# Row additions by chunk, normalisations in halves and a later transpose in the feed-forward stages of a cross-attention kernel

## The reference

```python
# layer 0: two cross attentions, then
h = _layer_norm(x, ln_mlp_scale, ln_mlp_offset)
h = gelu(h @ w_fc1 + b_fc1) @ w_fc2 + b_fc2          # 256 -> 1024 -> 256
return x + h
...
# layer 1: cross attention with latents, then
out = rmsnorm(attn_out, postnorm_w)
out = gelu(out @ mlp_w1 + mlp_b1) @ mlp_w2 + mlp_b2
return out + residual
...
# layer 2: cross attention, then
y = layer_norm(hidden, ln2_w, ln2_b)
return hidden + (gelu(y @ fc_w + fc_b) @ proj_w + proj_b)
...
# layer 3: attention over features, batch norm over all tokens, + x
```

## Time and profile before

| | |
|---|---|
| median of 3 timed runs | 1546.92 us (1546.78 to 1547.07) |
| the profiled execution's own time | 1547.88 us |
| its span, first to last instruction | 1546.1 us |
| TensorE busy | 1505.0 us, 97% |
| VectorE busy | 966.5 us, 63% |
| ScalarE busy | 872.6 us, 56% |
| Pool busy | 416.3 us, 27% |
| mean granted TensorE clock | 0.994 |

### The profile page before, as it was taken

How to read it: one execution, slowest core, us unless ns; L and a number is a source line. 1 busy time by engine, 2 the same in 40 slices (tenths; PEclk the granted TensorE clock), 3 DMA queues, 4 the chain that set the end, 5 groups by cost and what they waited for, 6 DMA issues and landing times. The chain is left out here.

```text
span 1546.1 us, 41347 instructions
## 1 busy us (share of the span) xinstructions
PE 1505.0 (97%) x17435; PEld 1314.3 (85%) x17435; DVE 966.5 (63%) x2125; ACT 872.6 (56%) x1635; POOL 416.3 (27%) x449
## 2 busy tenths in 40 slices
PE   9999999999999899999999999999999999999996
PEld 8888888888898788888888888978878988888864
DVE  7755564555666464645655576389996567865366
ACT  6563454454356454453353566577776667765476
POOL 3420210210211510210210124046764206542052
PEclk9999999999999899999999999999999999999998
DMA  6010010010010010010010000020002000001001
GB/s 216 29 43 2 28 43 1 29 42 2 29 42 2 28 42 2 29 43 2 29 43 29 29 9 21 1 84 2 4 28 83 1 29 3 30 2 28 9 21 55
DMA packets 17832, 46.20 MB, mean 30 GB/s; under 512 B 1360, under 2 KB 11616, under 8 KB 14704
## 3 DMA queue, kind: packets, MB, share of 16 engines
q1 hardware_dynamic: 13456, 39.33, 7.3%
q10 hardware_dynamic: 4192, 4.24, 0.8%
HBM read 39.37 MB, written 4.19 MB: 28 GB/s over the span
## 5 line engine op out<-in xcount | busy, mean ns | idle before, releaser
L174 PE MATMUL ps<-ch,W 128*128 128x512 f32 (+1 forms) x2517 | 583.0, 381 | 3.1 <-DVE ch L603 0.9
L174 PEld LDWEIGHTS ps<-ch,W 128*128 128x128 f32 x2517 | 439.0, 189 | 86.8 <-issue 2.2
L174 PEld LDWEIGHTS ps<-W,split_arena 128*128 128x128 f32 x3084 | 388.4, 188 | 23.5 <-issue 5.2
L174 PE MATMUL ps<-W,split_arena 128*128 128x256 f32 x3084 | 402.0, 283 | 3.3 <-DVE split_arena L1729 2.4
L1382 DVE TENSOR_REDUCE small<-ps 128x4 f32<-128x260 f32 x128 | 53.9, 421 | 240.5 <-PE ps L776 240.5
L1223 ACT ACTIVATE arena<-ps,hbias 128x512 f32<-128x512 f32 x128 | 87.8, 689 | 206.3 <-PE ps L174 205.3
L174 PE MATMUL ps<-W,ch 128*128 128x512 f32 (+1 forms) x1002 | 195.6, 353 | 0.4
L1208 ACT ACTIVATE arena<-ps 64x256 f32<-64x256 f32 x256 | 97.0, 379 | 170.1 <-PE ps L875 166.3
L174 PEld LDWEIGHTS ps<-W,ch 128*128 128x128 f32 x1002 | 162.5, 189 | 26.5 <-ACT arena L2217 0.9
L1729 DVE TENSOR_TENSOR split_arena<-arena,split_arena 128x512 fp32r<-128x512 f32 x96 | 72.2, 752 | 125.2 <-ACT split_arena L1761 115.5
L1409 DVE TENSOR_TENSOR x_sb<-ps,x_sb 128x512 f32<-128x512 f32 x128 | 86.5, 689 | 94.5 <-PE ps L174 94.4
(11 more groups left out here) (173 smaller groups left out, 2021.4 us busy)
## 6 DMA issues: line engine op xcount, KB each, us to landing
raw<-wpack SPq DMA_DIRECT2D x23, 1028.0 KB, 4.8
rows<-vb_in SPq DMA_DIRECT2D x8, 512.0 KB, 5.7
x_sb<-x_in SPq DMA_DIRECT2D x4, 512.0 KB, 9.6
arena<-ctxT SPq DMA_DIRECT2D x4, 512.0 KB, 10.1
spill<-x_sb ACTq DMA_DIRECT2D x1, 2048.0 KB, 11.7
arena<-spill ACTq DMA_DIRECT2D x1, 2048.0 KB, 9.4
arena<-ctx_tok SPq DMA_DIRECT2D x16, 128.0 KB, 2.1
out<-x_sb SPq DMA_DIRECT2D x7, 256.0 KB, 2.5
```

The costliest lines, as they stand in the source:

```text
L174: last = e.matmul(dst, lhs[a], rhs[b], start=start and n == 0, stop=stop and n == 2, skip_group_check=True)
```

## The change

Three things change, in stage 0 and stage 2 of the feed-forward stages.

1. Pool's row additions. Before, Pool took the power and the row addition of one chunk as a pair, in the first chunk of the stage. Now the powers come first, and the row addition of chunk c (all but chunk 0 of stage 0, and chunks 2 and 3 of stage 2) waits for the low part of the first unit of chunk c. The row of chunk 0 in stage 0 comes after the power of chunk 1.
2. In stage 0 the normalised rows `x` of chunks 2 and 3 are made in two halves, with a unit's low part between them.
3. In stage 0 the transposes of chunk 3 come a unit later (after "down" of unit 9, not of unit 8), and with them their evacuation, high part and low part.

```diff
@@ end of pool_attend
-            norm0.pool(e, 0, row("b_fc2"), 2)
+            norm0.pool_pow(e, 0, 2)
@@ mlp: own_norm, stage 0 (FT is 8)
-                {"dve": {1: [("x", 1)], 4: [("stats", 2)], 5: [("lo", 1), ("x", 2)],
-                         6: [("stats", 3)], 7: [("x", 3)], FT: [("lo", 2)], FT + 3: [("lo", 3)]},
-                 "pe": {3: [("T", 1)], 6: [("T", 2)], FT: [("T", 3)]},
+                {"dve": {1: [("x", 1)], 4: [("stats", 2)], 5: [("lo", 1), ("x_a", 2)],
+                         6: [("x_b", 2), ("stats", 3)], 7: [("x_a", 3)], FT: [("x_b", 3), ("lo", 2)], FT + 4: [("lo", 3)]},
+                 "pe": {3: [("T", 1)], 6: [("T", 2)], FT + 1: [("T", 3)]},
                  "act": {4: [(0, 1), (1, 1)], 5: [(2, 1), (3, 1)], 7: [(0, 2), (1, 2)], FT: [(2, 2), (3, 2)],
-                         FT + 1: [(0, 3), (1, 3)], FT + 2: [(2, 3), (3, 3)]}},
+                         FT + 2: [(0, 3), (1, 3)], FT + 3: [(2, 3), (3, 3)]}},
@@ mlp: pool(e, c, first, last)
                 if first and which == 0:
-                    for j in range(1, NCH):
-                        norm.pool(e, j, row(out_row), l)
+                    norm.pool_pow(e, 1, l)
+                    norm.pool_row(e, 0, row(out_row), l)
+                    norm.pool_pow(e, 2, l)
+                    norm.pool_pow(e, 3, l)
+                elif which == 0:
+                    e.wait_ge(s["gl"].sem, s["gl"].at(c * FT))
+                    norm.pool_row(e, c, row(out_row), l)
...
                 if first and which:
                     for j in range(front.left, NCH):
-                        norm.pool(e, j, norm.row)
+                        norm.pool_pow(e, j)
+                if which and norm.row is not None and c >= front.left:
+                    e.wait_ge(s["gl"].sem, s["gl"].at(c * FT))
+                    norm.pool_row(e, c, norm.row)
```

## The result

The changed kernel takes 1549.22 us (median of 22 runs, 1547.94 to 1549.96) against 1546.92 before (22 runs, 1546.15 to 1547.76): a ratio of 1.0013 [1.0007, 1.0019], taken over all runs (the two medians alone give 1.0015). It is 2.3 us slower, within the 0.2% that I called the same, but outside the range and on the other side of before than the predicted 1546.5.

The account below looks back on a forecast made before the run. TensorE, busy 1505.0 of 1546.1 us, was taken to bound the kernel, so only its waits could be gained. The terms 0.4 - 0.1 + 0.15 = 0.45 us took 1546.92 to 1546.5, range 1545.2 to 1547.9.

Parts of the forecast that it names:

- (a): Stage 0, Pool's row of chunk 0 moved behind the power of chunk 1: gain 0.4 us, bounds 0 and 0.6.
- (b): Stage 0, unit 6: low part starts 0.65 us earlier, so 0.64 of TensorE's wait before "down" goes.
- (c): Stage 0, unit 7: low part ends at 935.23, TensorE wants it at 935.58; no wait, 0.3 us spare.
- (d): Stage 0, unit 8: power of chunk 3 starts earlier, low part at 937.5; the 0.28 us wait goes.
- (e): Stage 0, unit 9: Pool's additions delay VectorE, undoing the gains of (b) to (d); 0.1 us loss, bounds gain 1.0, loss 0.8.
- (f): Stage 0, unit 12: chunk-3 low part comes behind the unit's, ScalarE's evacuation waits about 1.3 us; slack covers it: 0.
- (g): Chunks 2 and 3: moved row additions, then zeroing and key copies, cost 0; if all hit, both stages, 0.6 us.
- Stage 2: Row additions leave the first chunk and units 15 and 16 for units 16 and 24: gain 0.15 us, bounds 0 and 0.2.
- The signs that the prediction named for being right: Waits at units 6 and 8 shrink, over 1 us at unit 9, prompt chunk-3 power, line 875's 0.18 gone, additions wait-free.
- The second: Rival: unit 9 loses 0.8, chunks 2 and 3 up to 0.6, chunk 0's row gains nothing; around 1547.6 us, chance 0.17.
- the first: Rival: the port between Pool and VectorE doesn't matter in unit 9; gain at most 1.8, around 1545.5 us, chance 0.18.
- the third: Rival: Pool holds the port for whole bursts of additions, five times 1.5 us, 7.7 in all; 1554.6 us, chance 0.03.

Follow-up runs that it names:

- table_only: The kernel before with the new table alone (halves of x, later transposes of chunk 3), Pool's program as before; 1548.46 us, 1.0009 of before.
- row1_later: The changed kernel with Pool's row addition of chunk 1 waiting for the low part of unit 11 instead of unit 8; 1547.77 us, 1.0004 of before.
- zero_quiet: The changed kernel with Pool's eight zeroings moved from behind chunk 3's row addition to wait for unit 12's low part; 1548.02 us, 1.0004 of before.
- before_zero_late: The kernel before with only Pool's zeroings and the key copies behind them held until the low part of unit 25; 1548.47 us, 1.0008 of before.
- copy_two_inputs: The changed kernel with the copies of line 590 written as max(x, x), reading two SBUF inputs; 1547.43 us, 1.0003 of before.
- both: The changed kernel with chunk 1's row addition waiting for unit 11's low part and the zeroings for unit 12's; 1546.78 us, 0.9997 of before.

## Why the prediction was wrong

The lead, from row to row, gives each step its size.

- **(a)** 1.51 to 1.86 at line 875: 0.35 gained for 0.4, and its wait of 0.18 is gone. By `up` of unit 7 (930.24 against 928.63) it is 1.61 again: TensorE now waits 0.24 at line 776 for ScalarE, whose work there (line 1230) is only 1.52 ahead (900.56 against 899.04), and 0.38 for 0.30 at unit 0. Of the 0.4 only 0.10 is left. The step had that only as its lower bound.
- **(b)** 1.61 to 2.25 (932.50 against 930.25): 0.64, as forecast; the wait is gone.
- **(c)** No wait at unit 7, as forecast.
- **(d)** 2.25 to 2.60 (939.53 against 936.93): 0.35, the 0.28 and the slower restart. But the low part of unit 8 starts at 936.20, which with the 1.61 of lead is 937.81 on the clock of before, not 937.5. The power of chunk 3 began at 934.71 on that clock (forecast 934.6), ran 1.40, and VectorE still stood 0.97 for it. That is a term sized 0.3 too small.
- **(e)** From the start of the low part of unit 8 to "down" of unit 9 it is 5.49 (936.20 to 941.69), forecast 5.5. The total is right, but by luck, for the turns within are others. The step let Pool give way, with the fourth addition behind the pair (0.77 to 4.86), and priced the second half of `x` at 0.65. In the rows the four additions take 2.92, hardly more than alone, and are over at 939.88, while VectorE loses at the second half of `x` (1.35 for 0.73) and at the pair (1.83 for 1.29). So the row at 940.53 of before did not show the order of turns here: in table_only, where the pair stood first, Pool was held, and here, where the additions stood first, VectorE was. And the prediction's "the trace agrees" had rows for instructions with two inputs only; line 586 reads one tile and two small columns, and was held off too. `up` of unit 11 has a lead of 1.18. (b) to (e) together lost 0.43, where I had 0.1; the 0.3 between them is that of (d). row1_later shows that the additions are the cause: with them away, the same stretch to "down" takes 4.32 (937.61 to 941.93).
- **(f)** 0, right: the lead goes from 1.18 to 1.11 up to `up` of unit 18 (965.85 against 964.74).
- **(g)** This is the step that failed. Its first half is right: the additions of chunks 2 and 3, 3.34 us each, leave TensorE without a wait (the lead is 1.11 still at 967.25 against 966.14, and at 995.00 against 993.89). Its second half, "Pool's zeroing and key copies follow it, some 45 us later than before ... I take 0", asked only who waits for the zeroing, and not whom it would meet on VectorE. It cost 1.78 in the profile (lead 1.11 to -0.67). By zero_quiet the place of the zeroing costs 1.83 us of stage 0 or 0.89 (against the changed kernel's two profiles), by before_zero_late 0.90 without the rest of the diff. Without the 1.78 the median would have come to about 1547.4 (an estimate, 1549.22 - 1.78), within the range; zero_quiet, 0.96 above its before, stands at the range's upper end.
- **Stage 2.** The lead goes from -0.55 (1394.60 against 1395.15) to -0.36 (1422.65 against 1423.01): 0.19 for 0.15; "down" at 1421.57 runs 1.60.

In sum stage 0 lost 2.27 (0.35 - 0.25 - 0.43 - 0.07 - 1.78 - 0.09) and stage 2 gave 0.19: 2.08 of the 2.30 that the medians show. Between the two stages the lead also goes from -0.76 to -0.55, which these rows don't explain. The signs that the prediction named for being right were there, the wait of over 1 us at unit 9 too, and none of them looked at the copies. None of the rivals was it. The second, that the turns fall badly, has the right side and names the right kind of conflict, but its places (unit 9 by one more addition, waits in chunks 2 and 3) are not those. Against the first stands the wait at unit 9, against the third the additions without a wait. The trace of before held what I needed: the zeroing of 3.93 us from 943.00 and the copies at 945.96, stretched to 1.51, are on the timelines that I had read. The class was right, the range was not, since (g) had no bound of its own for the zeroing.

What stays open: why the four copies take 2.12 in one execution and 3.52 in the other of the same program. That it hangs on a small shift between two engines that take turns is argued, not shown. The spread of the timed runs is no help: it is 2.0 us for the changed kernel, but also 2.0 for zero_quiet and 2.5 for copy_two_inputs, in whose profiles TensorE has no wait at unit 27, and the profiles differ by 1.6 us before stage 0 begins. Nor do the runs settle whether `both` is faster than before.

## What to carry to other kernels

A step that is moved on one engine takes along everything that is queued behind it. For each such instruction look at who runs on the neighbouring engine at its new time, and not only at who waits for it. Where a Pool burst must go somewhere, look for a stretch where VectorE has no plain copies: at 950.72 of zero_quiet the eight memsets ran beside a pair of two-input subtractions (950.58), which kept its 1.29, and TensorE had no wait. Or write the instructions that it would meet in the form that memsets don't hold off (1.43 us for 3.52, at 1.43 for 0.90 in quiet). And a total that comes out right doesn't show that the order of turns behind it was right: look at each instruction's own time.

## What the runs showed of the hardware

- Pool's memsets, which read nothing, hold off VectorE's plain copies: four of 128x256 take 0.89 us alone and 1.51, 2.12, 3.52 or 4.82 in company (the first over the tail of the burst, the last with the end of Pool's additions in it). Both 2.12 and 3.52 came in executions of one program.
- The same copies written with two inputs take 1.43 us, in quiet and over the memsets.
- Pool's additions and VectorE's two-input subtractions hold each other off, and which side pays differs: four additions and a pair take 2.81 and 1.29 alone, 4.10 and 1.94 before, 2.92 and 1.83 in the changed kernel, 4.84 and 1.29 in table_only. In the last two the side that began first kept its time or nearly so.
- VectorE's scaling of rows (line 586), one SBUF input and two small ones, isn't free of it either: two take 0.73 us alone and 1.35 to 1.38 over Pool's additions.
- Pool's key copies (a cast) hold VectorE off as well: the four copies take 1.31 with 0.56 us of them on top, and the subtraction at 995.32 takes 1.08 for 0.69. Whether they are milder than memsets no run shows, as none laid a whole burst of them on the copies.
